# Two chained attentions in fp32 on one core: the second one's queries and keys stacked by term through DRAM

## What is computed

```python
x = x + _L0_conv_ref(_gn(x), ...)   # 8 heads of 16, 256 tokens of 16 features, relative position bias
x = x + _L1_conv_ref(_gn(x), ...)   # 16 heads of 16, over chunks of 64 tokens
# second one, for each image:
qkv = flat @ w_qkv.T                                  # 256 tokens x 256 -> 3 x (16 heads x 16)
k_cat, v_cat = [previous chunk, this chunk]           # queries of chunk c see keys of chunks c-1 and c
scores = einsum('bclhd,bcmhd->bchlm', q, k_cat) * 0.25
out = einsum('bchlm,bcmhd->bclhd', softmax(scores), v_cat).reshape(B, T, 256) @ w_out.T
```

## Time and profile before

| | us |
|---|---|
| median of 3 runs | 174.6 (174.55 to 175.02) |
| the profiled execution | 174.48 |
| its span, first to last instruction | 172.6 |

### The profile page before, as it was taken

How to read it: one execution, slowest core, us unless ns; L and a number is a source line. 1 busy time by engine, 2 the same in 40 slices (tenths; PEclk the granted TensorE clock), 3 DMA queues, 4 the chain that set the end, 5 groups by cost and what they waited for, 6 DMA issues and landing times.

```text
span 172.6 us, 4016 instructions
## 1 busy us (share of the span) xinstructions
PE 158.7 (92%) x1454; PEld 123.1 (71%) x1454; DVE 125.4 (73%) x339; ACT 102.2 (59%) x222; POOL 85.7 (50%) x131
## 2 busy tenths in 40 slices
PE   7788879799999999998999999999999999999872
PEld 7477668678797887986777747887678766575551
DVE  1736687966683894829998998978989779987220
ACT  1439329867765779877665837376483773353420
POOL 0310635779743548634863568425593276554000
PEclk9957699999999999999999999999999999999999
DMA  5419700000000000000000000000100001001001
GB/s 176 148 50 311 251 2 4 0 0 6 2 0 4 0 2 4 0 0 0 4 0 0 0 6 2 4 0 0 34 0 30 4 0 34 30 2 34 30 25 39
DMA packets 4979, 5.34 MB, mean 31 GB/s; under 512 B 440, under 2 KB 4920, under 8 KB 4960
## 3 DMA queue, kind: packets, MB, share of 16 engines
q1 hardware_dynamic: 4400, 4.74, 8.7%
q10 hardware_dynamic: 560, 0.35, 0.7%
HBM read 4.02 MB, written 1.06 MB: 29 GB/s over the span
## 4 chain that ended last, share of the span: by engine, by line
PE 77%; DVE 8%; ACT 5%; issue 4%; DMA 3%; ACTq 1%; DVEq 0%
PE bank L587 15%; PE bank L551 8%; PE bank L531 7%; PE bank L575 6%; PE bank L566 5%; PE bank L654 5%; PE bank L645 5%; PE bank L691 4%; PE bank L584 4%; PE bank L540 3%; PE bank L458 3%; DMA PT<-buckets 3%; PE bank L687 2%; PE bank L681 2%; PE bank L674 2%
## 5 line engine op out<-in xcount | busy, mean ns | idle before, releaser
L1192 ACT ACTIVATE PT<-bank 128x512 f32<-128x512 f32 x64 | 38.2, 599 | 30.2 <-PE bank L587 22.7
L340 POOL TENSOR_TENSOR Qk<-Qn,con 128x512 f32<-128x512 f32 x32 | 37.1, 1163 | 27.3 <-PE bank L587 26.9
L329 POOL TENSOR_SCALAR SB<-SB,NM 128x256 f32<-128x256 f32 x64 | 30.6, 491 | 14.9 <-DVE NM L956 14.4
L956 DVE CUSTOM_DVE_ANT_0 SB<-bank,Tk 128x256 f32<-128x256 f32 x64 | 24.4, 420 | 16.0 <-PE bank L551 16.0
L587 PE MATMUL bank<-Qk,Kf 128*128 128x512 f32 x64 | 32.6, 591 | 0.0
L968 DVE TENSOR_TENSOR D<-con,NM 128x512 fp32r<-128x512 f32 x32 | 28.9, 903 | 2.0 <-PE bank L587 1.9
L960 DVE TENSOR_REDUCE NM<-bank 128x4 f32<-128x512 f32 x32 | 21.9, 683 | 2.0 <-PE bank L566 1.8
L551 PE MATMUL bank<-KH,QM 128*128 128x256 f32 x64 | 19.9, 333 | 1.3 <-ACT QM L1174 0.7
L575 PE MATMUL bank<-con,SB 128*128 128x128 f32 x128 | 19.2, 272 | 0.0
L551 PE MATMUL bank<-KL,QM 128*128 128x256 f32 x64 | 17.0, 288 | 0.0
L566 PE MATMUL bank<-Km,Qs 128*128 128x512 f32 x32 | 16.8, 524 | 0.0
(11 more groups left out here) (155 smaller groups left out, 292.2 us busy)
## 6 DMA issues: line engine op xcount, KB each, us to landing
Tk<-bias_rows SPq DMA_DIRECT2D x4, 384.0 KB, 4.8
X<-x SPq DMA_DIRECT2D x4, 256.0 KB, 4.2
y<-Y SPq DMA_DIRECT2D x8, 128.0 KB, 1.7
Kf<-w_qkv SPq DMA_DIRECT2D x1, 768.0 KB, 7.4
Kf<-w_outb SPq DMA_DIRECT2D x1, 256.0 KB, 7.5
con<-consts ACTq DMA_DIRECT2D x1, 145.5 KB, 3.2
PT<-w_qk ACTq DMA_DIRECT2D x1, 128.0 KB, 4.0
PT<-buckets ACTq DMA_DIRECT2D x1, 64.0 KB, 4.5
```

The source lines that it names most:

```text
L329: last = nc.gpsimd.tensor_scalar(rows_of, rows_of, -1.0, NM[:, i % 2, 2 * u + nt:2 * u + nt + 1], ALU.mult, ALU.add)
L340: nc.gpsimd.tensor_tensor(Qk[:, idx % QRING, :].rearrange("p (a v q) -> p v a q", a=4, v=2), Qn[:, b % 2, g, c * CHUNK:(c + 1) * CHUNK].un ...
L956: last = V.tensor_tensor_reduce(SB[:, idx % SRING, nt * CH:(nt + 1) * CH], half, Tk[:, u, nt * P:nt * P + CH], 1.0, LOWEST, ALU.add, ALU.m ...
L1192: A.activation(PT[:, u, :], bank[Z_BANK + u % 2][:], ACT.Exp, scale=-SCALE if is_a(i) else SCALE).then_inc(p_ready, 1)
```

## The change

Units of A keep their instructions; the times at which some are hung change. For a unit of B:

- After the projection ScalarE writes the high part of queries and of keys (`QHL[:, 0]`, `KHL[:, 0]`), VectorE the low part (`[:, 1]`), one instruction each. SP stores each to DRAM (512 KB) and loads it again three times (256 KB each) into slots of 32 partitions: `Q3` gets high, low, high and `K3` high, high, low. A head pair's 32 rows then lie three times above each other, on 96 partitions, so that one product over 96 rows sums all three terms.
- GpSimd masks a block's queries to one head of the pair per half (`QP`, two instructions of 96 x 256), two steps ahead of the block, instead of L340.
- The scores of a block are four F32R products of 128 columns over 96 rows, one for each head pair, and are accurate. VectorE takes the maximum as before and then subtracts it from bank S into SB (128 x 512); bank S is held until that is done. TensorE transposes SB with four transpositions as in A. `Km`, `Qs`, `Qk`, `Kf`, `D`, `minus`, the second product and the diagonal go.
- The low part of the tokens moves to GpSimd, the copies of the values to ScalarE, with three buffers.
- Projections of B are hung four steps earlier, and attention one's end is moved so that its result is there in time.

`terms` runs on SP ahead of the output stores; `pair_queries` runs on GpSimd in step t for block t + 2; `below_max` runs on VectorE right behind the maximum of the same block.

```diff
-        TIMES_A = [(range(1, 2), (-6, -4, -3, -2)), (range(2, 3), (-5, -3, -2, -1)), (range(3, BATCH), (-8, -6, -4, -2))]
-        XT_B, GM_B, GV_B, Q_B, K_B, V_B = -9, -8, -7, -4, -3, -2
-        FINISH = [(range(UNITS - 1), (10, 13), (12, 15), (13, 16), (15, 18)),
+        TIMES_A = [(range(1, 2), (-6, -4, -3, -2)), (range(2, 3), (-5, -3, -3, -2)), (range(3, BATCH), (-9, -7, -7, -6))]
+        XT_B, GM_B, GV_B, Q_B, K_B, V_B = -13, -12, -11, -8, -7, -6
+        FINISH = [(IN_A, (9, 12), (14, 14), (15, 15), (17, 17)),
+                  (range(BATCH, UNITS - 1), (10, 13), (12, 15), (13, 16), (15, 18)),
                   (range(UNITS - 1, UNITS), (10, 13), (12, 15), (13, 16), (14, 17))]
...
+            def terms(b):
+                n, i = b % 2, BATCH + b
+                sp.wait_ge(q_ready, i + 1)
+                sp.dma_start(q_terms[b], QHL[:].bitcast(F32)).then_inc(q_written, 16)
+                sp.wait_ge(k_ready, i + 1)
+                sp.dma_start(k_terms[b], KHL[:].bitcast(F32)).then_inc(k_written, 16)
+                if b >= 2:
+                    sp.wait_ge(qk_ready, BLK * (b - 1))
+                sp.wait_ge(q_written, 16 * (b + 1))
+                for s, part in enumerate((0, 1, 0)):
+                    sp.dma_start(Q3[GRP * s:GRP * (s + 1), n].rearrange("p a g n -> p a (g n)"),
+                                 q_terms[b, :, part, :].rearrange("(a p) n -> p a n", p=GRP)).then_inc(q_loaded, 16)
+                if b >= 2:
+                    sp.wait_ge(s_done, BLK * (i - 1))
+                sp.wait_ge(k_written, 16 * (b + 1))
+                for s, part in enumerate((0, 0, 1)):
+                    sp.dma_start(K3[GRP * s:GRP * (s + 1), n].rearrange("p a g n -> p a (g n)").bitcast(F32),
+                                 k_terms[b, :, part, :].rearrange("(a p) n -> p a n", p=GRP)).then_inc(k_loaded, 16)
+            for b in range(BATCH):
+                terms(b)
 ...
+            def pair_queries(i, u):
+                if u == 0:
+                    pool.wait_ge(q_loaded, 16 * TERMS * (b + 1))
+                if idx >= QRING:
+                    pool.wait_ge(s_done, i * BLK + u - QRING + 1)
+                for v in range(2):
+                    last = nc.gpsimd.tensor_scalar(QP[0:ROWS, idx % QRING, :, v, :], Q3[0:ROWS, b % 2, :, g, c * CHUNK:(c + 1) * CHUNK],
+                                                   con[0:ROWS, C_SIDE + v:C_SIDE + v + 1], None, ALU.mult)
...
-                return nc.tensor.matmul(bank[S_BANK + u % 2][:], Qs[:, b % 2, g, c].rearrange("p v q -> p (v q)"), rhs,
-                                        start=True, stop=True)
+                for a in range(PAIRS):
+                    keys = K3[0:ROWS, b % 2, a, g, :]
+                    window = bass.AP(keys.tensor, keys.offset + first, [keys.ap[0], [step, 2], [1, CHUNK]])
+                    last = nc.tensor.matmul(bank[S_BANK + u % 2][:, a * P:(a + 1) * P],
+                                            QP[0:ROWS, idx % QRING, a].rearrange("p v n -> p (v n)"), window, start=True, stop=True)
...
-                nc.tensor.matmul(z[:], minus[:], D[:, (i * BLK + u) % DRING, :], start=True, stop=False, skip_group_check=True)
-                pe.wait_ge(qk_ready, b * BLK + u + 1)
-                w = WINDOW[c] * CHUNK
-                return nc.tensor.matmul(z[:], Kf[:, b % 3, g, w:w + 2 * CHUNK], Qk[:, (b * BLK + u) % QRING, :],
-                                        start=False, stop=True, skip_group_check=True)
+                below = SB[:, (i * BLK + u) % SRING, :]
+                for a in range(PAIRS):
+                    last = nc.tensor.transpose(z[:, a * P:(a + 1) * P], below[:, a * P:(a + 1) * P], ident)
...
+                elif u == 0:
+                    pe.wait_ge(k_loaded, 16 * TERMS * (i - BATCH + 1))
+                if not is_a(i):
+                    pe.wait_ge(qk_ready, idx - BATCH * BLK + 1)
+                if idx >= BATCH * BLK + 2:
+                    pe.wait_ge(subb_ready, idx - BATCH * BLK - 1)
...
+            def below_max(i, u):
+                dve.wait_ge(max_ready, idx + 1)
+                dve.wait_ge(z_done, idx - SRING + 1)
+                V.tensor_tensor(SB[:, idx % SRING, :].rearrange("p (h m) -> p h m", h=4),
+                                bank[S_BANK + u % 2][:].rearrange("p (h m) -> p h m", h=4),
+                                NM[:, i % 2, 4 * u:4 * u + 4].unsqueeze(2).to_broadcast([P, 4, P]), op=ALU.subtract).then_inc(subb_ready, 1)
```

More of the change, by code:

```diff
@@ L120, in build @@
         WoutK = sb("WoutK", [P, TT, P])
-        WQh, WQl, WKh, WKl = (sb(n, [P, 2, P], F32R) for n in ("WQh", "WQl", "WKh", "WKl"))
+        WQK = sb("WQK", [P, 4, 2, P], F32R)
+        WQh, WQl, WKh, WKl = (WQK[:, n] for n in range(4))
         WTh = sb("WTh", [P, CT, 3 * CH], F32R)
@@ L166, in build @@
         NM = sb("NM", [P, 2, 32])
-        DRING = 3
-        D = sb("D", [P, DRING, BW], F32R)
         OS = sb("OS", [P, 2, BW])
@@ L555, in scores_b @@
             def scores_b(i, u):
-                b = i - BATCH
+                b, idx = i - BATCH, (i - BATCH) * BLK + u
                 c, g = u // 2, u % 2
-                if u < 2:
-                    pe.wait_ge(km_ready, 2 * b + g + 1)
-                keys = Km[:, g, :, :]
-                if c == 0:
-                    rhs = keys[:, :, 0:CHUNK].unsqueeze(2).to_broadcast([P, 4, 2, CHUNK])
-                else:
-                    rhs = keys[:, :, (c - 1) * CHUNK:(c + 1) * CHUNK]
-                return nc.tensor.matmul(bank[S_BANK + u % 2][:], Qs[:, b % 2, g, c].rearrange("p v q -> p (v q)"), rhs,
-                                        start=True, stop=True)
+                first, step = ((0, 0), (0, CHUNK), (2 * CHUNK, -CHUNK), (2 * CHUNK, CHUNK))[c]
+                for a in range(PAIRS):
[3 more added lines that the diff above has]
+                                            QP[0:ROWS, idx % QRING, a].rearrange("p v n -> p (v n)"), window, start=True, stop=True)
+                return last
             def shifted_a(i, u):
@@ L612, in shifted @@
                 else:
-                    pe.wait_ge(d_ready, idx - BATCH * BLK + 1)
-                if u == 0 and not is_a(i):
-                    pe.wait_ge(kh_ready, i)
+                    pe.wait_ge(subb_ready, idx - BATCH * BLK + 1)
                 if idx >= 2:
@@ L862, in queries_keys @@
                 else:
-                    b = i - BATCH
-                    if which == 0:
-                        dve.wait_ge(qh_ready, i)
-                        if b >= 2:
-                            dve.wait_ge(s_done, BLK * (i - 1))
-                        for v in range(2):
-                            last = V.tensor_scalar(Qs[:, b % 2, :, :, v, :], Qn[:, b % 2].rearrange("p g (c q) -> p g c q", c=NCH),
-                                                   con[:, C_HALF + v:C_HALF + v + 1], None, ALU.mult)
-                        last.then_inc(q_ready, 1)
+                    f = bank[G_BANK if which == 0 else F_BANK]
+                    hl, ready, done = (QHL, qh_ready, q_ready) if which == 0 else (KHL, kh_ready, k_ready)
+                    dve.wait_ge(ready, i)
+                    V.tensor_tensor(hl[:, 1, :], f[:], hl[:, 0, :].bitcast(F32), op=ALU.subtract).then_inc(done, 1)
             def first_low(t):
@@ L1035, in _ @@
                     norm_x(2, t - 6)
-                for units, when in TIMES_A + [(IN_B, (XT_B, Q_B, K_B, V_B))]:
+                for units, when in TIMES_A:
                     for i in due(t, when[3] + 1, units):
@@ L1046, in _ @@
                         low_xr(i)
-                for i in due(t, GV_B + 2, IN_B):
-                    low_x(i - BATCH)
                 if t in (4, 5, 7):
                     low_weights((4, 5, 7).index(t))
-                for i in due(t, Q_B + 1, IN_B):
-                    queries_keys(i, 0)
-                for units, when in TIMES_A:
+                for units, when in TIMES_A + [(IN_B, (XT_B, Q_B, K_B))]:
                     for which in range(2):
@@ L1236, in _ @@
                         projected(i, step)
+                for i in due(t, V_B + 1, IN_B):
+                    value_rows(i)
                 for units, pv, t1, t2, out_step in FINISH:
@@ L1245, in _ @@
                             unnormalised(i, half)
-                for g in range(2):
-                    for i in due(t, g - 2, IN_B):
-                        head_keys(i, g)
 def kernel(x, L0_conv_w_in, L0_conv_w_qk, L0_conv_w_out, L0_conv_rel_bias, L1_conv_w_qkv, L1_conv_w_out):
```

170 lines of the change are left out of this document (73 added, 97 removed).

## The result

| | us |
|---|---|
| before, median of 4 | 174.81 (174.55 to 175.10) |
| changed, median of 4 | 182.19 (180.86 to 182.77) |
| ratio | 1.041, 95% interval 1.035 to 1.047 |
| the profiled execution, its span | 182.27, 180.5 |

The forecast was 166.4 us. The kernel got slower by 7.4 us, also above the range. Medians, ranges and ratios from here on leave out executions that fell into a slower state of the chip.

The account below looks back on a forecast made before the run. The prediction took TensorE's queue to bound B: 174.5 us, minus 13.1 for cheaper steps, plus 3.0 for waits in the units and 2.0 for the last steps, gives 166.4 us; its own range 163 to 169, overall 162 to 176.

Parts of the forecast that it names:

- The step of B on TensorE: Four F32R products and four transpositions take 0.91 us instead of 1.32; 32 steps save 13.1 us.
- the rival of products at the rate of plain float32: In B's steps, narrow F32R products run no faster than plain float32: step 1.29 us, total 174.5; chance 0.17.
- A full unit: Unit of B with projections: 17.6 us of TensorE work plus 1.7 of waits, 19.3 us.
- about 14.5 us a unit for 15.8: VectorE's work in a full unit of B was forecast at 15.8 us, against TensorE's 17.6, so not the bound.
- holding bank S: Rival in B: bank held until the subtraction makes VectorE the bound, units 20.5 us, total 171.7; chance 0.10.
- my 8 x 0.41 less 2.0: Last steps of B: 0.41 us saved per step, against 2.0 us extra taken for the 14 steps behind step 50.
- The projections of B come four steps earlier, the same instructions; ... taken as 0: Moving B's projections earlier costs nothing; the first image's XT following its residual sooner, 0 to 0.5 us each, taken as 0.
- Eight times two instructions at 0.49: GpSimd's masks per unit of B, priced at 0.49 us each; GpSimd 12.1 us a unit, uncovered showing 0.
- at nothing: Other edits, on GpSimd, ScalarE, projections and output stores, priced at 0; tokens' low part on GpSimd at 1.1 us.
- It fits with 1.8 us to spare: Stacking through DRAM takes 10.1 us of 11.9 from the keys' low part to a unit's first scores; no wait.
- the stacked terms come late: Rival: loads to 32 partitions at half rate, 3.2 us late per unit of B, total 179; chance 0.23.
- the clock at risk: Rival: TensorE's clock halves behind step 50, in steps without projections, costing up to 20 us; chance 0.03.

Follow-up runs that it names:

- x14: x10 with the first half of A's weights by values back at step 10 instead of 9; 173.24 us, ratio 0.987.
- x6: Changed kernel with masks on ScalarE and only one of three slots loaded per unit, still 96 rows, scores not the reference's; 174.08 us, ratio 0.994.
- x3: Kernel before with only A's new times, projections and closing steps; 179.56 us, ratio 1.029.
- x12: Kernel before with only A's closing steps as in the change; 179.10 us, ratio 1.023.
- x13: Kernel before with only A's projection times of units 2 and 3 as in the change; 177.88 us, ratio 1.014.
- x7: Changed kernel with each high part stored and loaded as soon as ScalarE has rounded it, low parts separately; 177.79 us, ratio 1.018.
- x10: Changed kernel with the edits of x7 and x9 together; 173.89 us, ratio 0.995.
- x9: Changed kernel with GpSimd's mask multiplying and then adding 0.0, two operations instead of one; 181.62 us, ratio 1.039.
- x11: x10 with A's values one step later in units 2 and 3; 174.50 us, ratio 0.997.
- x15: x14 with the rest of A's closing steps as in the kernel before, except the output at 17; 174.12 us, ratio 0.996.
- x16: x15 with A's values one step later in units 2 and 3; 173.65 us, ratio 0.994.
- x2: Changed kernel with one stacked term instead of three, 32 rows and one load each; 178.01 us from one execution.
- x4: Changed kernel with masks on ScalarE and one stacked term instead of three, 32 rows; 177.77 us, ratio 1.017.

## Why the prediction was wrong

**What held.** The step of B on TensorE: 0.88 measured for 0.91, so the rival of products at the rate of plain float32 is out. A full unit: 19.38 in the changed kernel (blocks 48 to 56; from 40 to 48 it is 21.07, at a clock of 0.92) and 19.2 in x14, for 19.3. VectorE: 0.685 and 0.692 for the two instructions, and about 14.5 us a unit for 15.8; holding bank S does not make it the bound (x6). The last stretch, from block 56, got 3.7 shorter, where my 8 x 0.41 less 2.0 gives 1.3: the 2.0 for the last steps was too much. 2.4 of it lie behind block 63 (19.56 to 17.11), since the transposed part of a block, which got cheaper, comes four steps behind its scores. One slip in the working: three projections, two halves of weights by values, two output products and 16 transpositions of 0.1 add up to 9.7, not 9.9, which moves neither the sum nor the range.

**"The projections of B come four steps earlier, the same instructions; ... taken as 0": the step that failed first.** I walked through the steps of B, and of A I only counted instructions, which are the same; for A's own new times the sum has no term at all. x3 shows 4.8 us for A's new times alone, x12 4.4 for the closing steps and x13 3.1 for the projections. TensorE takes its list in order, and work that is due before its input is ready makes it idle: 1.0 us for the output weights ahead of block 10 (x12), 2.5 us in all for VectorE to read the queries (x13). Of the 5.4 us that A lost from block 4 on, 3.7 are idle time (7.2 against 3.5), and 12 more matmuls, which now stand ahead of block 31 instead of behind it, are a part of the rest. The closing steps can also explain a third of the loss in the first unit of B: x12, with none of B's change, has 1.35 us more from block 32 to 40, where A's last image is finished, and x13 has none. Another 2.5 of the 4.0 is the wait ahead of block 40.

**"Eight times two instructions at 0.49": a price from the wrong row.** The subtraction that I took it from has two operations, the mask one. On GpSimd that is 0.476 against 0.919. It costs 3.9 us once the terms are early (x7 to x10). GpSimd's 20.38 us of 22.38 in the first unit look like the cause of the loss there, but aren't: with masks at half the price the unit takes 23.35 (x9, at a clock of 0.86), with slow masks and earlier terms 19.97 (x7). The tokens' low part, moved to GpSimd as another edit "at nothing", takes 1.28 us there instead of 1.1, and TensorE waits for it, 2.6 us in four times in x14 and never in the kernel before; no run moves it back.

**"It fits with 1.8 us to spare": mis-sized.** Forecast were 10.1 us from the keys' low part to the last load, measured 12.1, and TensorE had reached the end of its work at 85.5, 9.1 us after the low part's start, not 11.9. The rate was 313 GB/s in the sum; in B, from the 17th slice on, the page's row has 193 to 244 in the fullest ones, stores included. The store isn't what slows them: it had landed at 80.02 us, and behind it only loads run (changed kernel, GB/s in 40 slices of 82 to 88.5 us):

```profile
GB/s 189 239 240 252 240 202 214 227 227 214 240 227 214 214 227 214 202 202 202 202 202 189 202 214 240 214 177 176 151 114 76 88 63 25 0 0 0 0 0 0
```

From 80.9 to 86 us the mean is 217 GB/s with the DMA engines always busy, 0.7 of the 313. The waits were 3.1 at first and 7.6 us in all four units. That is the rival "the stacked terms come late", at 0.7 of the rate instead of half, and with less time at hand than it assumed. It was given 0.23, and half of that for slower than now.
The Trainium skill (SBUF, DMA port swizzle) has 32 neighbouring partitions reach half of the ports. The direction agrees, but no run here loads the same tensor to all 128 partitions, so whether the ports are the reason stays open.

**What no term held.** The masks' loss hides behind the late terms (x9 against x10). And a gap costs twice: behind the first two the granted clock fell, to 0.50 and 0.57. In the first two units of the changed kernel it is 0.92 in the mean; that is 16% of 22.38 and 21.07 us at half speed, which by my estimate costs up to 3.5 us. A gap isn't the only thing that goes ahead of a fall: in x10's profiled execution the clock is at 0.59 from 120 to 124 us and at 0.55 from 124 to 128, and between block 32 and there TensorE has no gap of 0.9 us or more; what released that fall stays open. The forecast had the clock at risk only in the steps without projections, and in the changed kernel it stood at 1.00 there. The Trainium skill (TensorE: Matmul & The Clock Gate, PE-mode transpose) would have put it in danger there; four of the eight products of a bare step are transpositions, and the page of the changed kernel has 9 in every slice of that stretch. No run here has transpositions alone.

**The sum in its right form**, for x14 against before: A +4.1, handover +0.2, first unit of B +0.7, two full units -4.2 (forecast -4.0), rest -3.6, and 0.6 less before block 0. That is -3.4 us in the span of this execution, x14's fastest, of which 0.9 lies ahead of block 4; by the medians it is -1.5. Of the 15.8 us between forecast and result, x6 brings back 8.1 (terms and masks) and x3 shows 4.8 (A's times); for the 2.9 that are left no run was made. Still open is how to place the projections of A so that they end in time and cost nothing; x11, x15 and x16 didn't find it.

## What to carry to other kernels

When a change moves work to earlier steps, walk through the steps it lands in as carefully as through those it leaves; two lines of due times cost 4.8 us here, and could have been timed alone in one run. When undoing a suspect gives nothing, undo it together with the next one before letting it go: here the slow masks showed only once the data came in time. A busy engine isn't the cause of a loss by being busy; see whether the loss goes when it is relieved. For a round trip through DRAM, send what is ready first: splitting the high part from the low one brought 4.4 us for eight more transfers.

## What the runs showed of the hardware

- GpSimd's `tensor_scalar` on 96 x 256 float32 takes 0.92 us with one operation and 0.475 with two (x6, x9), contiguous or in pieces of 64, to float32 or F32R. Adding 0.0 about halves it.
- Four products over 32 rows and the four transpositions behind them take 1.17 us a step, over 96 rows 0.88, both at a granted clock of 1.00 (x2 and x4 against the changed kernel); over the whole kernel that was 3.7 us (x4 against x6). The transpositions, the same in both, go from 0.37 to 0.59, the products from 0.51 to 0.58. The Trainium skill (TensorE: Matmul & The Clock Gate, Why this matters for your kernels) says that a single product with 32 rows takes as long as one with 128; for this alternation the runs say it takes longer, and why was not tested.
- Four F32R products of 128 columns over 96 rows take 0.51 us from start to start, four of 256 columns over 128 rows 0.56: half the columns save next to nothing.
- Loads of 256 KB to 32 partitions, with nothing else on the DMA engines and these always busy, move 217 GB/s in the mean (changed kernel, 80.9 to 86 us); the inputs move 313 from 12 to 20 us.
